# Grouped attention: POOL's query sum ahead of the last pair of scatters, key split, exponentials and one turn moved, and the row turns issued twice

## Chip, cores and metric

One core of one Trainium2 chip runs the whole program. The metric is the device time of one execution in microseconds (us).

## The reference, cut to what matters

The model is two layers on x of shape (16, 512, 128). The change touches only the attention half of the first layer's feed-forward block (`_L0_ffn_ref`), with the router behind it:

```
h = rmsnorm(layernorm(x), ln1_w)
q, k, v = h @ Wq (16 heads of 8), h @ Wk, h @ Wv (4 heads of 8), rope on q and k
attn = softmax(causal(q k^T / sqrt(8)))        # each k, v head serves 4 q heads
h = clip(x + (attn v) @ Wo, -100, 100)
flat = rmsnorm(h, ln2_w); probs = softmax(flat @ Wr); top 2 of 8 experts
```

Behind it come the experts' products, a second attention with eight blocks, and a ternary feed-forward. All sixteen sequences of 512 tokens go through each stage before the next stage begins.

## The kernel before, in words

`grouped_attention` (lines 52 to about 1115) is written by hand for five engines: `pe_program`, `act_program`, `pool_program`, `dve_program` and `sp_program` give each engine one order of work, and semaphores tie them. It is a software pipeline over the NB = 16 sequences. Each program loops `for b in range(-1, NB + 2)` and inside it over eight steps `s`. In one step PE computes the scores of one pair of heads of sequence b and, 11 pairs ahead, the scores from which DVE takes the row maxima. Other parts of the step serve other sequences: c = b + 1 (maxima turned and stored), c2 = b + 2 (its q and k are rotated, split in three bf16 parts and stored), c3 = b + 3 (statistics, normalising, projection), p = b - 1 (output projection, clip, rows for the experts) and r = b - 2 (router and scatters).

What sets the order around the change:

- PSUM: `S` has six banks, used as three pairs in turn. `score(n, part)` and `max_scores(m, part)` alternate, three of each in a step, so each of them waits until the pair was emptied: by `exponentials` on ScalarE or by `take_max` on DVE. `M` is one bank for all small products (`turn_x`, `project_q`, `sum_k`, `turn_o`, `turn_h`, `route` and so on); `bank_free` waits for whoever reads the one before.
- The query chain: `cosines` and `sines` (DVE, lines 775 and 781) fill `rotA` and `rotB`, `rotate` (POOL, line 659) adds them, `split_q` (DVE, lines 804 to 808) makes two bf16 parts and `third_q` (POOL, line 663) the last. The key chain: `sum_k` (PE), `copy_sum` (ScalarE), `split_k` (DVE, lines 793 to 797), `third_k` (POOL, line 668).
- SP's queue, in this order for c2: `store_q`, which waits for `third_q` (lines 1028 to 1032), `store_k` (1038 to 1040), `load_q` (1047) when q's stores have landed, `load_k` (1054) when k's have. They go through DRAM, to bring heads on the partitions that the scores need. PE waits for both loads in `max_scores` at step 4 of b, where the maxima of sequence b + 2 begin.
- POOL also normalises (`scales`, `normalise`), scales the residual, clips, makes the rows for the experts and issues eight indirect DMAs for each sequence (`scatter`, line 716: two choices of expert, four tiles of 128 tokens), in pairs at steps 4, 5, 6 and 7.

Of the kernel before, what the change touches and what calls it, by code (L numbers as in the profile page):

```python
# [46 lines left out]
def grouped_attention(nc, C, XT, H, G, R, NB):  # L47
# [15 lines left out]
    with ExitStack() as ctx:  # L63
# [154 lines left out]
        def pe_program(pe):  # L218
# [86 lines left out]
            def turn_h(r):  # L305
                bank_free()
                pe.wait_ge(row_ready, r + 1)
                for t in range(NT):
                    last = pe.transpose(M[:, t * P:(t + 1) * P], rows[:, r % 2, t, 0:P],
                                        C["ident"][:, :])  # L310
                last.then_inc(h_turned, 1)
                taken[0] = (h_copied, r + 1)
# [116 lines left out]
            for b in range(-1, NB + 2):  # L429
                p, c, c2, c3, r = b - 1, b + 1, b + 2, b + 3, b - 2  # L430
                for s in range(8):
# [16 lines left out]
                        turn_o(b, 0)  # L448
                    if s == 5 and exists(c):
                        turn_max(c)  # L450
                    if s == 6 and exists(b):
                        turn_o(b, 1)
                    if s == 7 and exists(c3):
                        project_qs(c3)
                    if scanning:
                        max_scores(m, 0)
                    if weighing and s % 2 == 0:
                        pe.wait_ge(probs, 6 * group + 6)
                        if group:
                            pe.wait_ge(o_copied, group)  # L460
                        weigh(group, FIRST[0])
# [31 lines left out]
        def act_program(act):  # L493
# [88 lines left out]
            for b in range(-1, NB + 2):  # L582
                p, c, c2, c3, r = b - 1, b + 1, b + 2, b + 3, b - 2
                for s in range(8):
                    n = 8 * b + s + 1
                    attending = 0 <= n < 8 * NB
                    if s == 0 and exists(p):
                        copy_o(p, 2)
                    if s == 2 and exists(p):
                        copy_o(p, 3)  # L590
                    if s == 4 and exists(b):
                        copy_o(b, 0)
                    if s == 6 and exists(b):
                        copy_o(b, 1)
                    if attending:
                        exponentials(n, 0)
                    if s == 1 and exists(r):
                        copy_h(r)
                    if s == 5 and exists(c):
                        copy_max(c)  # L600
                    if attending:
                        exponentials(n, 1)
                    if s == 0 and exists(c2):
                        copy_sum(c2)
                    if s == 2 and exists(c2):
                        copy_v(c2)
                    if s == 2 and exists(r):
                        ratios(r)
                    if s == 3 and exists(p):
                        copy_yT(p)  # L610
                    if s == 5 and exists(c3):
                        copy_xT(c3)
                    if attending:
                        exponentials(n, 2)
                    if s == 6 and exists(p):
                        squares(p)

        def pool_program(pool):
# [109 lines left out]
            pool.memset(v12[:, :, :, :, VD:VD + 1], 1.0).then_inc(zeroed, 1)  # L728
            first_residual()
            residual(1)  # L730
            for b in range(-1, NB + 2):
                p, c2, c3, r = b - 1, b + 2, b + 3, b - 2
                for s in range(8):
                    if s == 0 and exists(c2):
                        rotate(c2)
                    if s == 1 and exists(c2):
                        third_q(c2)
                        third_k(c2)
                    if s == 3 and 2 <= c3 < NB:
                        scales(c3)  # L740
                        normalise(c3)
                    if s == 5 and 1 <= c3 < NB:
                        residual(c3)
                    if s == 5 and exists(p):
                        clip(p)
                    if s == (5 if p == NB - 1 else 6) and exists(p):
                        make_rows(p)
                    if s == 4 and exists(r):
                        weigh_rows(r)
                    if s >= 4 and exists(r):  # L750
                        scatter(r, s // 6, ((0, 1), (2, 3))[s % 2])
            for half in range(2):
                pool.wait_ge(scattered[half], 16 * 2 * NT * (NB // 2))

        def dve_program(v):
# [226 lines left out]
            for b in range(-1, NB + 2):  # L982
                p, c, c2, c3, r = b - 1, b + 1, b + 2, b + 3, b - 2
                for s in range(8):
# [3 lines left out]
                        combine(p, 2)  # L988
                    if s == 2 and exists(p):
                        combine(p, 3)  # L990
                    if s == 3 and exists(r):
                        place(r)
                    if s == 4 and exists(b):
                        combine(b, 0)
                    if s == 6 and exists(b):
                        combine(b, 1)
                    if s == 7 and exists(c3):
                        sines(c3)
                    if scanning:
                        take_max(m, 0)  # L1000
                    if scanning:
                        take_max(m, 1)
                    if s == 0 and exists(c2):
# [6 lines left out]
                        rotate_k(c3)  # L1010
                    if scanning:
                        take_max(m, 2)
                    if s == 0 and exists(c2):
                        split_k(c2)
                    if s == 1 and exists(r):
                        choose(r)
                    if s == 2 and 2 <= c3 < NB:
                        measure(c3)
                    if s == 3 and exists(c):
                        shift(c)  # L1020
            make_plan()

        def sp_program(sp):
# [2568 lines left out]
```

## Time and profile before

| | us |
|---|---|
| median of 3 runs | 3304.95 (3292.81 to 3307.48) |
| the profiled execution, whole | 3274.55 |
| its span | 3272.8 |
| PE busy in the span | 2983.6 |
| DVE busy | 2458.4 |
| ScalarE busy | 2327.2 |
| POOL busy | 2020.2 |

Busy time is the sum over instructions; the span runs from the first to the last instruction. The profiled execution is some 30 us shorter than the median of the runs. Grouped attention is the stretch from about 540 to 1340 us.

### The profile page before, as it was taken

What the parts mean: (1) busy time and instruction counts of PE and PEld (TensorE: products, weight loads), DVE (VectorE), ACT (ScalarE), POOL (GpSimd) and SP (SyncE); (2) the same over time, 40 slices, a digit from 0 to 9 for tenths busy, and PEclk for the clock granted to TensorE, in tenths of its full rate; (3) what the DMA queues carried; (4) which work ended last, traced back from release to release, by engine and by line L of the source; (5) the groups of instructions that cost most, each with busy time, mean ns of one, the idle gap of its engine ahead of it and who ended that gap; (6) DMA issues with size and microseconds to landing.
All of it is one profiled execution on the core that took longest, in us unless ns stands there. A gap on an engine that the chain in (4) does not pass through costs nothing. (4 is left out here: it accounts for less than half of the span.)

```text
span 3272.8 us, 66154 instructions
## 1 busy us (share of the span) xinstructions
PE 2983.6 (91%) x22290; PEld 1870.3 (57%) x22290; DVE 2458.4 (75%) x6927; ACT 2327.2 (71%) x3599; POOL 2020.2 (62%) x2351
## 2 busy tenths in 40 slices
PE   6999997898888988488679999999999999999979
PEld 3554554344444443377536666666666666666658
DVE  5666666888777774366468888888888888888867
ACT  5787773466555657243258999999999999999933
POOL 4454453355555543466547787878787878787745
PEclk8999998899999999699889999999999999999989
DMA  4444434312331220475330000000000000000001
GB/s 122 123 111 102 127 98 94 66 46 58 68 68 45 65 68 18 119 241 162 98 103 1 7 11 1 16 1 16 1 16 1 16 1 16 1 7 11 1 14 40
DMA packets 178774, 178.31 MB, mean 54 GB/s; under 512 B 18667, under 2 KB 159174, under 8 KB 178341
## 3 DMA queue, kind: packets, MB, share of 16 engines
q1 hardware_dynamic: 169348, 157.14, 18.6%
q0 software_dynamic: 9088, 16.94, 1.5%
q8 instruction: 179, 2.93, 0.4%
q14 instruction: 159, 1.29, 0.1%
HBM read 99.82 MB, written 75.95 MB: 54 GB/s over the span
## 5 line engine op out<-in xcount | busy, mean ns | idle before, releaser
L3092 PE MATMUL lb_FF<-lb_h,lb_w 128*128 128x512 f32 x1024 | 501.9, 593 | 0.0
L3325 DVE TENSOR_SCALAR lb_z<-lb_M,lb_mv,lb_rstd 128x128 f32<-128x128 f32 x1024 | 345.2, 399 | 3.3 <-POOL lb_rstd L3247 3.0
L3210 ACT ACTIVATE lb_h<-lb_H,lb_prm 128x512 f32<-128x512 f32 x512 | 326.0, 695 | 2.6 <-PE lb_H L3083 2.6
L3247 POOL TENSOR_TENSOR lb_rstd<-lb_rstd,half 128x4 f32<-128x4 f32 x256 | 260.5, 1018 | 36.9 <-issue 0.9
L3077 PE MATMUL lb_H<-lb_x1s,lb_w 128*128 128x512 f32 x512 | 273.6, 534 | 0.0
L1661 POOL TENSOR_SCALAR_AFFINE_SELECT da_PT<-da_PT 128x1024 f32<-128x1024 f32 x128 | 146.2, 1148 | 192.3 <-ACT da_PT L1587 192.3
L3092 PEld LDWEIGHTS lb_FF<-lb_h,lb_w 128*128 128x128 f32 x1024 | 193.3, 189 | 91.1 <-issue 61.5
L566 ACT ACTIVATE ga_PT<-ga_S 128x384 f32<-128x384 f32 x256 | 111.6, 488 | 184.5 <-PE ga_S L377 184.4
L3317 DVE BATCH_NORM_STATS2 lb_stats<-lb_M 128x6 f32<-128x128 f32 x1024 | 227.2, 285 | 14.3 <-PE lb_M L3036 8.9
L1592 ACT ACTIVATE da_PT<-da_SY 128x1536 f32<-128x1536 f32 x128 | 185.2, 1447 | 72.7 <-PE da_SY L1441 71.8
L2405 POOL DMA_INDIRECT moe_ys<-moe_y,moe_dest x156 | 160.7, 1030 | 111.2 <-DVE moe_y L2287 65.1
L3078 PE MATMUL lb_H<-lb_x1s,lb_w 128*128 128x512 f32 x512 | 202.6, 396 | 0.0
L3083 PE MATMUL lb_H<-lb_x1s,lb_w 128*128 128x512 f32 x512 | 201.8, 395 | 0.0
L1453 PE MATMUL da_O<-da_PT,da_V 128*32 128x128 f32 (+2 forms) x3584 | 191.5, 326 | 2.6 <-DVE da_oT L1824 2.1
L3265 POOL CAST lb_x1s<-lb_x 128x512 fp32r<-128x512 f32 x128 | 78.2, 611 | 175.4 <-DVE lb_x L3350 175.4
L819 DVE TENSOR_REDUCE ga_bm<-ga_S 128x8 f32<-128x1024 f32 x128 | 156.1, 1219 | 36.9 <-PE ga_S L401 32.5
L3258 POOL TENSOR_TENSOR lb_xs<-H,lb_xs 128x512 fp32r<-128x512 f32 x128 | 169.2, 1321 | 18.4 <-issue 0.2
L816 DVE TENSOR_REDUCE ga_bm<-ga_S 128x8 f32<-128x1024 f32 x128 | 156.1, 1220 | 31.4 <-PE ga_S L401 29.4
L3268 POOL TENSOR_TENSOR lb_x1s<-lb_x,lb_x1s 128x512 fp32r<-128x512 f32 x128 | 163.5, 1278 | 20.5 <-issue 20.5
L3279 POOL TENSOR_TENSOR lb_y<-lb_ao,H 128x512 f32<-128x512 f32 x128 | 165.5, 1293 | 16.2 <-ACT lb_ao L3197 13.2
L3291 POOL TENSOR_TENSOR lb_y<-lb_ff,lb_x 128x512 f32<-128x512 f32 x128 | 164.6, 1286 | 8.4 <-PE lb_M L3036 5.3
L3191 ACT ACT_TABLE_LOAD x131 | 168.1, 1283 | 2.3
(445 smaller groups left out, 8786.6 us busy)
## 6 DMA issues: line engine op xcount, KB each, us to landing
moe_w<-experts_dram SPq DMA_DIRECT2D x39, 384.0 KB
da_qT<-da_stq SPq DMA_DIRECT2D x64, 192.0 KB, 3.8
da_kT<-da_stk SPq DMA_DIRECT2D x64, 192.0 KB, 4.4
moe_x<-moe_xs SPq DMA_DIRECT2D x39, 260.0 KB
tc_g<-moe_ys SPq DMA_DIRECT2D x32, 256.0 KB
ga_q<-ga_stq SPq DMA_DIRECT2D x20, 384.0 KB, 6.1
lb_split<-moe_parts SPq DMA_DIRECT2D x8, 896.0 KB
da_stq<-da_parts SPq DMA_DIRECT2D x16, 384.0 KB, 2.4
```

The lines of the kernel that those rows point to most:

```text
L1453: last = pe.matmul(O[32 * c:32 * c + 32, q0:q0 + cols], V[:, (n // 4) % 2, j, 2 * (n % 4) + c % 2, :], PT[:, (2 * n + c // 2) % RING, c % ...
L1592: act.activation(PT[:, n % RING, :, 512:HEAD_COLS], SY[:, :, :].rearrange("p a n -> p (a n)").rearrange("p (i n) -> p i n", i=2), ACT.Exp, ...
L3077: pe.matmul(H[:, k % 2, :], w1[:, 0, k, :], x1s[:, 0, :], start=True, stop=False)
L3078: pe.matmul(H[:, k % 2, :], w1[:, 1, k, :], x1s[:, 0, :], start=False, stop=False)
L3083: pe.matmul(H[:, k % 2, :], w1[:, 0, k, :], x1s[:, 1, :], start=False, stop=True).then_inc(h_filled, 1)
L3092: pe.matmul(FF[:, :], w2[:, k, :], h[:, k, :], start=(k == 0), stop=(k == KC - 1)).then_inc(ff_filled, 1)
L3191: act.preload_act_table_set("gelu_apprx_tanh_and_others")
L3210: act.activation(h[:, k, :], H[:, k % 2, :], ACT.Gelu_apprx_tanh, bias=col(FB1 + k, i)).then_inc(h_ready, 1)
L3247: pool.tensor_tensor(out[:, :], out[:, :], C["half"][:, 0:NT], ALU.pow).then_inc(done, 1)
L3258: pool.tensor_tensor(part_of_x(i, 1), state(i), part_of_x(i, 0).bitcast(F32), ALU.subtract).then_inc(xs_ready, 1)
L3317: v.bn_stats(stats[:, t, :], M[:, t * P:(t + 1) * P])
L3325: last = v.tensor_scalar(z[:, t, :], M[:, t * P:(t + 1) * P], mv[:, t, 0:1], rstd[:, t:t + 1], ALU.subtract, ALU.mult)
```

## The change

It moves work within four programs. On PE `turn_h` issues its four transposes twice, with the same inputs and the same output, and `turn_o(b, 1)` goes behind the first `max_scores` of step 6. On ScalarE the third group of exponentials goes ahead of `copy_yT` and `copy_xT`. On POOL `rotate` of a sequence runs in step 7 of the pass before, between the last two pairs of scatters, and not after them; `third_k` goes ahead of `third_q`, `clip` ahead of `residual`, the second pair of scatters from step 5 to step 4, the third from step 6 to step 7. On DVE `split_k` goes behind the first maximum of step 1, `combine(b, 1)` behind the first maximum of step 6; `measure` and `sines` are written a step later and a step earlier.

```diff
@@ turn_h (PE)
-                for t in range(NT):
+                for t in [*range(NT)] * 2:
                     last = pe.transpose(M[:, t * P:(t + 1) * P], rows[:, r % 2, t, 0:P],
@@ pe_program
-                    if s == 6 and exists(b):
-                        turn_o(b, 1)
                     if s == 7 and exists(c3):
                         project_qs(c3)
                     if scanning:
                         max_scores(m, 0)
+                    if s == 6 and exists(b):
+                        turn_o(b, 1)
@@ act_program
+                    if attending:
+                        exponentials(n, 2)
                     if s == 3 and exists(p):
                         copy_yT(p)
                     if s == 5 and exists(c3):
                         copy_xT(c3)
-                    if attending:
-                        exponentials(n, 2)
@@ pool_program
+            rotate(1)
             for b in range(-1, NB + 2):
                 p, c2, c3, r = b - 1, b + 2, b + 3, b - 2
                 for s in range(8):
-                    if s == 0 and exists(c2):
-                        rotate(c2)
                     if s == 1 and exists(c2):
                         third_q(c2)
+                    if s == 0 and exists(c2):
                         third_k(c2)
...
+                    if s == 5 and exists(p):
+                        clip(p)
                     if s == 5 and 1 <= c3 < NB:
                         residual(c3)
-                    if s == 5 and exists(p):
-                        clip(p)
...
-                    if s >= 4 and exists(r):
-                        scatter(r, s // 6, ((0, 1), (2, 3))[s % 2])
+                    if s == 4 and exists(r):
+                        scatter(r, 0, (0, 1))
+                    if s == 4 and exists(r):
+                        scatter(r, 0, (2, 3))
+                    if s == 7 and exists(r):
+                        scatter(r, 1, (0, 1))
+                    if s == 7 and 2 <= c3 < NB:
+                        rotate(c3)
+                    if s == 7 and exists(r):
+                        scatter(r, 1, (2, 3))
@@ dve_program
+                    if s == 3 and 2 <= c3 < NB:
+                        measure(c3)
                     if s == 3 and exists(r):
                         place(r)
                     if s == 4 and exists(b):
                         combine(b, 0)
+                    if scanning:
+                        take_max(m, 0)
+                    if s == 1 and exists(c2):
+                        split_k(c2)
                     if s == 6 and exists(b):
                         combine(b, 1)
-                    if s == 7 and exists(c3):
-                        sines(c3)
-                    if scanning:
-                        take_max(m, 0)
...
-                    if s == 0 and exists(c2):
-                        split_k(c2)
                     if s == 1 and exists(r):
                         choose(r)
-                    if s == 2 and 2 <= c3 < NB:
-                        measure(c3)
                     if s == 3 and exists(c):
                         shift(c)
+                    if s == 6 and exists(c3):
+                        sines(c3)
```

## Rows read from the trace of the kernel before

**Rows 1.** Windows by stage: us, busy us of each engine, granted clock, DMA share, GB/s
```profile
540.00:1340.00 800.00, 676.91 (x7788) 338.02 (x7784) 591.04 (x1259) 448.13 (x1070) 390.42 (x537) 0.91 0.25 58
```

**Rows 2.** Windows of one sequence and of two stretches in it
```profile
812.30:859.60 47.30, 42.37 (x489) 20.96 (x488) 37.32 (x80) 27.94 (x70) 25.73 (x35) 0.93 0.27 61
...
828.90:835.10 6.20, 6.17 (x50) 2.66 (x52) 5.16 (x22) 2.28 (x4) 0.06 (x1) 0.50 0.84 173
...
837.40:842.30 4.90, 4.18 (x70) 2.33 (x67) 4.60 (x18) 3.44 (x9) 2.25 (x6) 1.00 0.18 35
```

**Rows 3.** Timeline of DVE, steps 0 and 1: start, us, line, operation [idle before, releaser]
```profile
821.32 1.23 DVE L819 TENSOR_REDUCE ga_bm<-ga_S 128x8 f32<-128x1024 f32 x1 [1.00 <-PE ga_S L401]
823.29 0.43 DVE L804 CAST ga_partsQ<-ga_rotA 128x512 bf16<-128x512 f32 x1 [0.74 <-POOL ga_rotA L659]
...
825.50 0.99 DVE L793 CAST ga_partsK<-ga_restK 32x512 bf16<-32x512 f32 x1
826.57 0.68 DVE L795 TENSOR_TENSOR ga_restK<-ga_restK,ga_partsK 32x512 f32<-32x512 f32 x1
827.33 0.42 DVE L797 CAST ga_partsK<-ga_restK 32x512 bf16<-32x512 f32 x1
827.67 1.21 DVE L816 TENSOR_REDUCE ga_bm<-ga_S 128x8 f32<-128x1024 f32 x1
```

**Rows 4.** Timeline of PE, the same steps
```profile
819.77 0.38 PE L401 MATMUL ga_S<-g_k,g_q 48*128 48x384 bf16 x4
...
823.15 0.66 PE L309 MATMUL ga_M<-ident,ga_rows 128*128 128x128 f32 x4
...
825.64 0.39 PE L377 MATMUL ga_S<-ga_q,ga_k 51*128 51x384 bf16 x4 [0.50 <-DVE ga_bm L823]
...
828.93 0.40 PE L377 MATMUL ga_S<-ga_q,ga_k 51*128 51x256 bf16 x2 [1.69 <-DVE ga_bm L816]
```

**Rows 5.** Timeline of POOL: first two scatters of four, sum, thirds
```profile
817.05 1.11 POOL L716 DMA_INDIRECT moe_xs<-ga_rows,slot  x1 [0.80 <-issue]
818.47 0.96 POOL L716 DMA_INDIRECT moe_xs<-ga_rows,slot  x1 [0.30 <-issue]
...
821.98 1.28 POOL L659 TENSOR_TENSOR ga_rotA<-ga_rotA,ga_rotB 128x512 f32<-128x512 f32 x1
825.07 1.15 POOL L663 TENSOR_TENSOR ga_partsQ<-ga_rotB,ga_partsQ 128x512 bf16<-128x512 f32 x1 [1.81 <-DVE ga_partsQ L808]
827.82 1.14 POOL L668 TENSOR_TENSOR ga_partsK<-ga_restK,ga_partsK 32x512 bf16<-32x512 f32 x1 [1.60 <-DVE ga_partsK L797]
```

**Rows 6.** Timeline of SP's queue, in this sequence and the first
```profile
826.25 0.38 SPq L1028 DMA_DIRECT2D ga_stq<-ga_partsQ  x1
...
830.35 0.90 SPq L1047 DMA_DIRECT2D ga_q<-ga_stq  x2
...
565.03 0.37 SPq L1028 DMA_DIRECT2D ga_stq<-ga_partsQ  x1
...
569.09 0.95 SPq L1047 DMA_DIRECT2D ga_q<-ga_stq  x2
```

**Rows 7.** Two lines of DVE by source: ns min/median/max, first and last start
```profile
L793 DVE CAST ga_partsK<-ga_restK x15: 951/993/1001, 564.3 to 1203.7; 32x512 bf16<-32x512 f32 x15
...
L2297 DVE COPY moe_weight<-moe_x x39: 155/160/451, 1369.3 to 1611.2; 128x4 f32<-128x4 f32 x39
```

**Rows 8.** Timeline of PE at steps 3 and 4, and in the first sequence
```profile
841.15 0.28 PE L377 MATMUL ga_S<-ga_q,ga_k 51*128 51x256 bf16 x2 [0.33 <-DVE ga_bm L816]
...
843.42 0.39 PE L347 MATMUL ga_S<-identb,half_masks 64*128 64x256 bf16 x4
...
578.26 0.61 PE L347 MATMUL ga_S<-identb,half_masks 64*128 64x256 bf16 x4 [5.13 <-DMA ga_k<-ga_stk]
```

**Rows 9.** Timeline of PE at step 6 and at the stage's end
```profile
806.61 0.63 PE L281 MATMUL ga_M<-ident,ga_oT 128*128 128x128 f32 x4 [0.37 <-ACT ga_oT L527]
...
1326.99 1.09 PE L309 MATMUL ga_M<-ident,ga_rows 128*128 128x128 f32 x4 [6.10 <-POOL ga_rows L686]
```

More of the change, by code:

```diff
@@ L990, in dve_program @@
                         combine(p, 3)
+                    if s == 3 and 2 <= c3 < NB:
+                        measure(c3)
                     if s == 3 and exists(r):
```

## The prediction

> **What bounds the kernel now.** I read the windows by stage first [rows 1]: the diff touches grouped_attention alone, and that stage holds 800.00 us of the 3272.8 us span. In it TensorE (PE) is busy 676.91 us, VectorE (DVE) 591.04, ScalarE 448.13, POOL 390.42. No engine is full; PE and DVE hand six PSUM banks back and forth, and each waits for the other in turn.
>
> Then the windows of one sequence [rows 2]. A full one (eight steps of the inner loop, s = 0 to 7) takes 47.30 us with a mean granted clock of 0.93. Where the missing share lies the next row shows: from 828.90 to 835.10 the granted clock is 0.50, the lower of the two levels (1.2 GHz), with PE busy 6.17 of 6.20 us. At full clock that is 3.1 us of work.
>
> DVE's timeline ahead of that stretch [rows 3] is one chain. The second maximum of step 0 waits 1.00 us for PE and ends at 822.55; the query split waits 0.74 for POOL's sum; then DVE runs without a gap: split_q, third maximum, split_k from 825.50 to 827.67, and only then step 1's first maximum, which ends at 828.89. PE's timeline [rows 4] shows its other side: PE waits 0.50 us for the third maximum and 1.69 us for that first one, and the half clock follows. POOL's timeline [rows 5]: four scatters from 817.05 on (two are shown), then the sum, 821.98 to 823.26, then the third bf16 parts of q and k. SP's timeline [rows 6]: q is stored from 826.25, loads of q from 830.35, those of k behind them.
>
> **The change, step by step, in a full sequence.** All times are on the clock of the sequence shown. Two moves are none: measure at the end of step 2 and at the head of step 3 is the same place in DVE's order, and so is sines from step 7's head to step 6's tail. They cost 0.
>
> *Sum ahead of the last two scatters.* POOL ends its second scatter at 819.43; the sum then runs to about 820.7 (1.28 us) and is 2.5 us earlier. The wait of 0.74 is gone. PE's completions also come late beside scatters: the last matmul of the second maximum starts before 820.15, yet DVE starts at 821.32 [rows 3, 4], and with three scatters in this stretch gone I give DVE 0.9 of that 1.00 back. split_q starts at about 821.4 instead of 823.29, PE at step 1 at 822.0 instead of 822.6.
>
> *Row turns twice.* Four transposes more. Their spacing in the group of four at 823.15 (0.66 us for four) [rows 4] bounds this by 0.66; PE overlaps them, and I take 0.44. PE gets to step 1's first maximum at 823.6 and DVE can start on it at 824.25, 0.6 us after it is free. So the double turn lies on this chain, but the whole chain is not the end, as below.
>
> *split_k behind step 1's first maximum.* That maximum runs at 824.25 to 825.5 instead of 827.67, so PE's 1.69 us wait goes. What is late next is the second maximum: it is now behind split_k. Here a term shrinks. split_k is 0.99 + 0.68 + 0.42; its first cast takes 0.99 in all 15 sequences [rows 7], although the same cast on four times the partitions takes 0.43 [rows 3], and POOL's third_q (825.07 to 826.22) runs beside it [rows 5]. third_q now stands behind third_k and can't run there, so I take the cast at 0.42: split_k lasts 1.6, to 827.1, the second maximum to 828.3, and PE, done at 827.4, waits 0.9 instead of 1.69 + 0.50.
> The Trainium skill (SBUF — State Buffer, "Who interferes with whom") says that VectorE casts and GpSimd hold a shared port pair as an exclusive lock; the 0.99 agrees. The same rule speaks against the change, since the last two scatters now run beside split_q's casts.
>
> What a row of this kind shows: a DVE copy in the stage that gathers experts, beside scatters, takes 0.160 us in the median and 0.451 at most [rows 7], 0.3 more. Two casts beside two scatters are 0 to 0.6 us, and the 0.6 us that DVE waits for PE hides it. If a cast waits for a whole scatter (0.96) it is up to 1.5, of which 0.9 shows.
>
> *third_k ahead of third_q: the term that I take to decide.* SP stores q first. q's third part was ready at 826.22 and is now behind third_k, which waits for split_k: 827.1 + 1.14 + 1.15 = 829.4, that is 3.2 us later. Store to load takes 3.6 (4.1 before, when SP was still issuing k's stores), so the loads start at 833.1 instead of 830.35: +2.8 us. PE needs q and k of the new sequence at step 4's first maximum, 843.42 before [rows 8]. How long the loads take is seen in the first sequence, where PE did wait for them: load of q issued 569.09, PE freed at 578.26 after a wait of 5.13 [rows 6, 8], 9.1 us. Before, they were thus there at 839.5, 3.9 us early. After, at 842.2. Meanwhile DVE's chain brings PE to that point 2.8 us sooner, at 840.6. So PE waits about 1.6 us for DMA at step 4, and of the 2.8 us won in steps 0 to 3 only 1.2 are left there. Behind that point PE, not DVE, is late, so its small waits for DVE in steps 4 and 5 shrink (one of 0.33 at step 3 is shown [rows 8]); I take 0.23 for them, with bounds 0 and 0.5.
>
> *turn_o and combine of step 6 behind the maximum.* PE's wait of 0.37 for ScalarE's copy [rows 9] goes, since the maximum fills it; combine ends ahead of the projection that needs its bank. -0.37.
>
> *Scatters of step 5 next to those of step 4; exponentials ahead of copies; clip ahead of residual; thirds on POOL.* ScalarE and POOL have room (448 and 390 of 800 us) [rows 1]; the late completions move from step 6 to steps 4 and 5. Bounds -0.4 to +0.4, value 0, because DVE has both signs of slack there.
>
> Sum without the clock: -1.2 - 0.23 - 0.37 = -1.8 us a sequence.
>
> *The clock.* The old half-clock stretch lay behind waits of 0.50 and 1.69 us. The new one at step 1 (0.9) may be too short for it; between 837.40 and 842.30, with a wait of 0.33 [rows 8], the clock stayed at 1.00 [rows 2]. But the DMA wait of 1.6 us is about as long as the 1.69 and has DVE-bound waits ahead of it. I expect the half clock behind it in most sequences. Six us of it cost 3.1, and step 4 on is PE's; three cost 1.5. Allowing for some sequences without it I take 1.3. What it gives back at steps 1 and 2 is in the 2.8 us already, and ends in the DMA wait.
>
> Net -0.5 us for each of the 12 sequences whose steps hold all of this (b = 2 to 13), -6. The two before lack scatters and router: 0. The first, b = -1, is pure loss: split_k starts 1.1 us later, q is stored at 569.4 instead of 565.03, and PE already waits for these loads [rows 8]; bounds 0 and +4.3, taken +3.5, near the upper end since a DVE idle of about 1 us is all that lies between. In the drained end the turn of the last sequence takes 1.09 us at half clock [rows 9]; twice it is +0.9. Sum: -6 + 3.5 + 0.9 = -1.6, call it -2.
>
> The profiled execution took 3274.55 us, 1.75 around its span; it becomes 3273. The median of the runs is 3304.95, 30 us above it, so the same -2 gives **3303**.
>
> **The rivals.**
> 1. *The loads come in time.* If PE's lag or the DVE chain is otherwise than I have it, 3 us a sequence stay: 12 x 3.3 = -40, +4.4 at the ends, 3269. For: before, the margin was 3.9 us. Against: +2.8 on one side and -2.8 on the other overrun it.
> 2. *The DMA wait is there but the clock holds.* 12 x -1.8 + 4.4 = -17: 3288. For: a wait of 0.33 us did nothing. Against: the 1.69.
> 3. *Slower.* The half clock comes at step 4 with its whole six us (2.8 lost, after 0.3 of slack) and split_q's casts wait for scatters, which puts the loads 0.9 later: -1.8 + 2.8 + 0.9 = +1.9 a sequence, 12 x 1.9 + 4.4 = +27: 3332. It decides from the point where clock and casts together cost over 1.8 us. For: PE is busy 6.17 of 6.20 us in the old stretch, all of it stretched work. Against: the cast row's 0.3 us.
> 4. *Nothing is moved that matters*, the waits only change names: 3305 (+-5).
>
> **How the numbers follow.** A measurement of this kernel can tell about 0.5%, 16.5 us, from no change. Chances: my case 0.40, rival 1 0.20, rival 2 0.17, rival 3 0.13, rival 4 0.10. Faster by over 0.5%: rival 1, most of rival 2 and a little of mine, 0.32. Slower: rival 3 and some of mine, 0.18. Within: 0.50. My case's own range is 3290 to 3316. The range takes in rival 1 and goes half way to rival 3: 3266 to 3322.
>
> **What would show it.** PE's rows at step 4 show waits for DMA, up to 1.6 us each (right), or none (rival 1). split_k's first cast is 0.42 (right) or 0.99. The row turn has eight transposes and the maximum of step 1 starts ahead of split_k. SP's first store of q stands behind third_k's end by 1.2 us. PE's granted clock: 0.5 at step 4 rather than at step 1. The first load wait grows from 5.1 to about 9 us. Wrong would be a stage of 800 us that shrinks by over 20 or grows by over 15.

## The result, and the profile after

| | before | after |
|---|---|---|
| median of 7 runs, same chip | 3292.81 us (3284.39 to 3307.48) | 3321.56 us (3311.59 to 3328.55) |
| profiled execution, whole | 3274.55 | 3328.55 |
| its span | 3272.8 | 3326.8 |
| grouped attention, to DVE's plan for the experts | 539.8 to 1347.0: 807.2 | 540.6 to 1387.5: 846.9 |

The ratio is 1.008, 95% interval 1.006 to 1.0099: 28.8 us slower by the medians. The forecast was practically no change (3303); the time lies just inside the edge of its range (3322), and the direction was missed. The two profiled executions are extremes, before's below all seven of its runs and after's the longest of its seven, so their difference of 54 us overstates the change.

Where the 54 us lie: 5.3 ahead of the first exponentials (48.8 became 54.1), 32.0 in sequences 0 to 13, 5.6 in the last two. From the last scores to the end of the experts' products it is 14.2 more (323.9 became 338.1), and the rest gives some 3 back. DVE's plan, by which the table ends the stage, comes 3.1 us sooner behind the last scores, but SP's first load of the experts' rows 2.6 later (1355.58 and 1401.81 us), so the drained end gives nothing back. The code of the experts is unchanged, and the same stretch takes 332.8 to 339.7 us in the six other profiles from chips as slow as this one: the profile of before was short there, and most of the 18 us by which it undercuts its median can lie there rather than in grouped attention.

A full sequence takes 48.98 us in the mean, 46.78 before. By steps, in the mean of the twelve full sequences (b = 2 to 13; a step runs from PE's masks for one pair of scores to the next), and beside it the time lost to the half clock, which is the stretch times the share of the clock not granted:

| us a sequence | before | after | forecast |
|---|---|---|---|
| steps 0 to 3 | 25.3 | 24.0 (-1.3) | -2.8 |
| step 4, with the wait for the loads | 5.7 | 8.6 (+2.9) | +1.6 wait, +1.3 clock |
| steps 5 and 6 | 10.6 | 11.2 (+0.6) | -0.6 |
| step 7 | 5.1 | 5.1 | 0 |
| lost to the half clock, steps 0 to 3 | 2.7 | 2.4 | |
| the same, step 4 | 0 | 2.1 | |
| the same, steps 5 and 6 | 0 | 0.6 | |

The half clock takes 5.1 us of a full sequence after and 2.7 before. These 2.4 us more are about as much as the whole sequence is longer (2.2).

The windows of the changed kernel's stage, of a stretch at step 4 of the sequence that starts at 1134.06, and of another full sequence (from 983.47) with a stretch at its steps 2 and 3 (columns as in [rows 1, 2]):
```profile
540.60:1387.50 846.90, 713.90 (x7852) 361.40 (x7852) 591.68 (x1273) 446.49 (x1070) 395.70 (x543) 0.86 0.24 55
1158.90:1165.70 6.80, 5.85 (x38) 3.16 (x40) 3.50 (x6) 1.15 (x3) 5.75 (x8) 0.51 0.04 13
983.50:1034.50 51.00, 46.84 (x496) 23.55 (x492) 36.81 (x80) 27.89 (x68) 25.73 (x35) 0.83 0.25 57
994.90:1008.50 13.60, 13.25 (x108) 6.71 (x110) 9.49 (x39) 4.25 (x10) 3.39 (x8) 0.50 0.79 161
```
The counts differ by 64 matmuls, the second row turns (the window of [rows 1] ends 7 us before the stage does); DVE's work is the same. The granted clock of the stage fell from 0.91 to 0.86, and PE's busy time rose with it. The second row is the half clock at its new place, step 4. The last row is the half clock at the old place: it did not go. PE's wait at the head of step 2 is 0.98 to 1.08 us in all twelve full sequences, and in eight of them the half clock sets in with it or just behind it, as in the sequence from 983.47; in the other four, the one from 1134.06 among them, it does not:
```profile
995.25 0.61 PE L347 MATMUL ga_S<-identb,half_masks 64*128 64x256 bf16 x4 [1.03 <-DVE ga_bm L828]
...
1145.81 0.39 PE L347 MATMUL ga_S<-identb,half_masks 64*128 64x256 bf16 x4 [1.01 <-DVE ga_bm L828]
```
So the rows that follow show a sequence in which the forecast for steps 0 to 3 came true, and they are not typical in that.

DVE's timeline, steps 0 and 1 of a sequence whose step 0 starts at 1134.06 (816.56 in [rows 3]):
```profile
1137.69 1.23 DVE L828 TENSOR_REDUCE ga_bm<-ga_S 128x8 f32<-128x1024 f32 x1 [0.32 <-PE ga_S L401]
1138.83 0.42 DVE L813 CAST ga_partsQ<-ga_rotA 128x512 bf16<-128x512 f32 x1
...
1141.83 1.23 DVE L825 TENSOR_REDUCE ga_bm<-ga_S 128x8 f32<-128x1024 f32 x1 [0.71 <-PE ga_S L401]
1142.97 0.41 DVE L802 CAST ga_partsK<-ga_restK 32x512 bf16<-32x512 f32 x1
...
1144.55 1.21 DVE L828 TENSOR_REDUCE ga_bm<-ga_S 128x8 f32<-128x1024 f32 x1
```
The split of q follows its maximum without the old wait of 0.74 and the wait of 1.00 is 0.32. The first cast of split_k takes 0.41 where it took 0.99 [rows 3], and 0.40 to 0.41 in all 15 sequences: POOL is no longer on third_q beside it. That is the shared port of the Trainium skill (SBUF — State Buffer, "Who interferes with whom"), and here row and page agree. The cast at 1138.83 runs beside the scatter of 1138.58 (below) and takes 0.42: I had the same rule speak against the change, and this row shows nothing of it.

POOL's and SP's timelines, the same sequence:
```profile
1137.14 1.27 POOL L659 TENSOR_TENSOR ga_rotA<-ga_rotA,ga_rotB 128x512 f32<-128x512 f32 x1
1138.58 0.99 POOL L716 DMA_INDIRECT moe_xs<-ga_rows,slot  x1 [0.17 <-issue]
...
1144.71 1.14 POOL L668 TENSOR_TENSOR ga_partsK<-ga_restK,ga_partsK 32x512 bf16<-32x512 f32 x1 [3.85 <-DVE ga_partsK L806]
1145.82 1.16 POOL L663 TENSOR_TENSOR ga_partsQ<-ga_rotB,ga_partsQ 128x512 bf16<-128x512 f32 x1
```
```profile
1147.00 0.38 SPq L1037 DMA_DIRECT2D ga_stq<-ga_partsQ  x1
1150.78 0.83 SPq L1056 DMA_DIRECT2D ga_q<-ga_stq  x2
1151.66 0.95 SPq L1063 DMA_DIRECT2D ga_k<-ga_stk  x2
```
q's third part waits behind k's, so q is stored 12.94 us after the start of step 0 (9.69 in [rows 6]) and loaded from 16.72 (13.79). The k loads land at 1159.76. What that meets on PE, and the same in the first sequence:
```profile
1155.63 0.28 PE L377 MATMUL ga_S<-ga_q,ga_k 51*128 51x256 bf16 x2 [0.64 <-DVE ga_bm L825]
...
1157.67 0.63 PE L281 MATMUL ga_M<-ident,ga_oT 128*128 128x128 f32 x4 [0.29 <-ACT ga_oT L527]
1159.85 0.61 PE L347 MATMUL ga_S<-identb,half_masks 64*128 64x256 bf16 x4 [1.55 <-issue]
...
1160.82 1.93 PE L410 MATMUL ga_O<-ga_PT,ga_v 128*32 128x512 f32 x8
...
584.36 0.61 PE L347 MATMUL ga_S<-identb,half_masks 64*128 64x256 bf16 x4 [10.06 <-DMA ga_k<-ga_stk]
```
Inside a sequence the wait bears the name "issue", since it is PE's queue that holds it; that it ends 0.09 us after the landing gives its cause. PE was released in this way in 11 of the 15 sequences, counted by that distance. In the other four the half clock had held PE up for 13.7 us of steps 2 and 3, so that it came 2.0 to 2.9 us behind the landing. In the mean of the full sequences the wait is 1.4 us, at most 3.47. Behind it four mask matmuls take 0.61 where they take 0.39 at full clock [rows 8].

In the stretch behind it POOL now issues four scatters in a row, the first and the last of which are shown, and DVE waits for matmuls:
```profile
1160.92 1.23 DVE L825 TENSOR_REDUCE ga_bm<-ga_S 128x8 f32<-128x1024 f32 x1 [0.83 <-PE ga_S L401]
1168.85 1.23 DVE L825 TENSOR_REDUCE ga_bm<-ga_S 128x8 f32<-128x1024 f32 x1 [1.82 <-PE ga_S L401]
```
```profile
1162.80 1.10 POOL L716 DMA_INDIRECT moe_xs<-ga_rows,slot  x1 [0.29 <-POOL ga_rows L696]
...
1166.74 0.96 POOL L716 DMA_INDIRECT moe_xs<-ga_rows,slot  x1 [0.30 <-issue]
```
Before, the second pair came 3.95 us behind the end of the first, with the residual and the clip between them:
```profile
849.71 0.95 POOL L716 DMA_INDIRECT moe_xs<-ga_rows,slot  x1 [0.31 <-issue]
...
854.61 1.07 POOL L716 DMA_INDIRECT moe_xs<-ga_rows,slot  x1 [0.17 <-issue]
```

### The profile page after: what moved, and what is told of

The parts are those of the page before. It is cut to its first block and busy times, and to the rows that moved or that the text cites. A ratio compares the mean times of both kernels' runs of the same rounds, so it can differ in the third digit from the quotient of the medians.

```text
span 3326.8 us, 66282 instructions
## 1 busy us (share of the span) xinstructions
PE 3017.5 (91%) x22354; PEld 1891.8 (57%) x22354; DVE 2450.4 (74%) x6927; ACT 2326.4 (70%) x3599; POOL 2022.9 (61%) x2351
```

## Experiments

One thing has to be known for all of them. The comparisons fell on chips of two kinds, with one session on each chip. On some the kernel before takes 3293 to 3296 us (A below: two of the experiment chips, and the first comparison), on the others 3227 to 3229 (B). Each ratio is against before on its own chip. The same two programs were profiled on both kinds. The rows show DVE's first and second maximum: busy us and mean ns, then the idle time before them. The kernel before on A, then on B:
```profile
L816 DVE TENSOR_REDUCE ga_bm<-ga_S 128x8 f32<-128x1024 f32 x128 | 156.1, 1220 | 31.4 <-PE ga_S L401 29.4
L819 DVE TENSOR_REDUCE ga_bm<-ga_S 128x8 f32<-128x1024 f32 x128 | 156.1, 1219 | 36.9 <-PE ga_S L401 32.5 <-remote 3.4
```
```profile
L819 DVE TENSOR_REDUCE ga_bm<-ga_S 128x8 f32<-128x1024 f32 x128 | 156.2, 1220 | 25.8 <-PE ga_S L401 23.4
L816 DVE TENSOR_REDUCE ga_bm<-ga_S 128x8 f32<-128x1024 f32 x128 | 156.1, 1220 | 17.0 <-PE ga_S L401 15.1
```
The changed kernel on A, then on B:
```profile
L825 DVE TENSOR_REDUCE ga_bm<-ga_S 128x8 f32<-128x1024 f32 x128 | 156.5, 1223 | 75.4 <-PE ga_S L401 70.2 <-remote 3.1
L828 DVE TENSOR_REDUCE ga_bm<-ga_S 128x8 f32<-128x1024 f32 x128 | 156.3, 1221 | 40.6 <-PE ga_S L401 39.0
```
```profile
L825 DVE TENSOR_REDUCE ga_bm<-ga_S 128x8 f32<-128x1024 f32 x128 | 156.5, 1223 | 53.2 <-PE ga_S L401 51.2
L828 DVE TENSOR_REDUCE ga_bm<-ga_S 128x8 f32<-128x1024 f32 x128 | 156.3, 1221 | 35.9 <-PE ga_S L401 33.5
```
The operations take the same on both; DVE waits longer for PE on A. In A's traces such a wait can end long after the matmul. Where DVE stands idle for a maximum whose last matmul ended within 1.5 us after a scatter's start, it starts 0.74 us behind that end in the mean of before, 0.63 in the change and 1.48 in e16, by 3.3 at most; with no scatter that near, 0.04 to 0.06. In B's twelve traces it is 0.04 everywhere. Below, this is called a late completion.

All results (stage, to DVE's plan, and mean full sequence from each kernel's own profile, us; the kernel before has 807.2 and 46.78 on A):

| | kind | ratio to before, 95% | stage | sequence |
|---|---|---|---|---|
| change, first comparison | A | 1.008 [1.006, 1.0099] | 846.9 | 48.98 |
| change again (e7) | B | 1.0048 [1.0035, 1.0061] | 810.3 | 46.66 |
| before again, one run (e8) | B | | 811.6 | 47.14 |
| k first alone (e2) | B | 1.0032 [1.0018, 1.0046] | 805.8 | 46.36 |
| split_k alone (e4) | B | 0.9981 [0.9971, 0.9991] | 800.5 | 46.14 |
| q first (e1) | B | 0.9899 [0.988, 0.9917] | 769.5 | 43.79 |
| q first, again (e12) | B | 0.9905 [0.9889, 0.9922] | | 43.95 |
| q first, third time (e16) | A | 1.0045 [1.0029, 1.0061] | 829.5 | 48.22 |
| keep clock (e3) | B | 0.9998 [0.9987, 1.0009] | 797.9 | 45.51 |
| keep clock, again (e14) | B | 0.9992 [0.9981, 1.0002] | | 45.38 |
| single turn (e5) | B | 1.0035 [1.0023, 1.0047] | 805.1 | 46.34 |
| q first, single (e6) | B | 0.988 [0.9866, 0.9894] | 760.2 | 42.94 |
| the same, again (e13) | B | 0.9879 [0.986, 0.9898] | | 42.94 |
| the same, third time (e17) | A | 1.0038 [1.0019, 1.0056] | 820.8 | 47.91 |
| e6 with split_k later (e9) | A | 1.0105 [1.0087, 1.0124] | 844.7 | 49.45 |
| e6 with the sum last (e10) | A | 1.0132 [1.0099, 1.0165] | 860.6 | 50.69 |
| the same, again (e18) | A | 1.0139 [1.0113, 1.0165] | 857.9 | 50.62 |
| e6 with early statistics (e11) | A | 0.996 [0.9942, 0.9979] | 803.3 | 45.55 |
| the same, again (e15) | B | 0.9856 [0.9838, 0.9874] | 753.0 | 42.18 |

**Order of the thirds.** The change, but q's third part ahead of k's (e1, e12, e16):
```diff
-                    if s == 1 and exists(c2):
-                        third_q(c2)
                     if s == 0 and exists(c2):
+                        third_q(c2)
+                    if s == 1 and exists(c2):
                         third_k(c2)
```


> The changed kernel with third_q ahead of third_k again. Theory A (q's third part, behind split_k and third_k, stores q late, PE waits for the loads at step 4 and falls to half clock there): q is stored at about 5 us earlier in each sequence, no DMA wait at step 4, a full sequence takes 43.5 to 45 us in place of 48 to 51, ratio to before 0.983 to 0.992. Theory B (the double turns, the scatters next to each other and the sum between scatters cost it): the sequence stays at 47.5 us or more and the ratio at 1.003 to 1.008.

On B it is 1% faster than before, and 1.5% (3241.81 to 3197.9 us, 44 us) faster than the change. These two times come from two chips of kind B, where before took 3228.53 and 3226.83. POOL and SP in it, then PE at step 4, in the sequence whose step 0 starts at 812.83:
```profile
819.65 1.16 POOL L663 TENSOR_TENSOR ga_partsQ<-ga_rotB,ga_partsQ 128x512 bf16<-128x512 f32 x1
823.33 1.14 POOL L668 TENSOR_TENSOR ga_partsK<-ga_restK,ga_partsK 32x512 bf16<-32x512 f32 x1 [2.52 <-DVE ga_partsK L806]
```
```profile
820.84 0.38 SPq L1037 DMA_DIRECT2D ga_stq<-ga_partsQ  x1
825.86 0.90 SPq L1056 DMA_DIRECT2D ga_q<-ga_stq  x2
```
```profile
836.31 1.07 PE L281 MATMUL ga_M<-ident,ga_oT 128*128 128x128 f32 x4 [0.29 <-ACT ga_oT L527]
837.31 0.60 PE L347 MATMUL ga_S<-identb,half_masks 64*128 64x256 bf16 x4
```
q is stored 2.5 us ahead of the start of k's third part, and PE goes into step 4 without a wait for the loads (the 1.07 and 0.60 show that its clock is half here too, with no wait longer than 0.64, 0.38 and 0.29 us in the 3 us ahead; it is so in five of the twelve full sequences, and the stage's mean is 0.92). The repetition on B:

> The changed kernel with third_q ahead of third_k, again. On a chip with late completions: if the late store is the whole cause of the harm, 0.988 to 0.993 as on the other chip; if the late completions carry part of it, steps 0 and 2 to 5 keep some of it and the ratio is 0.996 to 1.004. On a chip without them 0.989 to 0.991 again.

0.9905: the same. The first edit alone, in the kernel before (`third_k(c2)` ahead of `third_q(c2)`, e2):

> The kernel before with third_k ahead of third_q and nothing else. Theory A: q's third part comes 3.3 us later, which the old margin of about 3.9 us at step 4 just holds in most sequences, and split_k's first cast falls from 0.99 to 0.42 us; the first sequence's wait for loads grows by 3.3 us. Ratio 0.996 to 1.004. If the order of the thirds costs by itself, whatever the margin: ratio 1.006 or more, with DMA waits at step 4.

1.0032, clearly slower, though the sequences of its profile, 8 us below its median, are no longer than before's: without the earlier sum and split_k, PE arrives later, and its wait for the loads at step 4 is 0.8 us in the mean of the full sequences, with seven of over 1 us among the 15; in e7 the mean is 1.15. Its front, from the stage's start to the first exponentials, is 54.4 us. So the order of the thirds costs 0.3% by itself on B and 1.5% once the rest of the change brings PE there earlier.

**The clock behind the wait.** The change, with the four transposes that precede the wait issued four times, so that PE works where it waited (e3, e14):
```diff
-                for t in range(NT):
+                for t in [*range(NT)] * (4 if g == 0 else 1):
```


> The changed kernel with the turn of step 4 (turn_o of group 0) issued four times instead of once, which fills 1.3 us of PE's wait for the loads with transposes. Theory A with the clock as its larger term: PE still reaches the first maximum of the new sequence when the loads have landed, but at full clock; steps 4 and 5 lose 2 to 3 us less in a sequence, ratio to before 0.997 to 1.003. If the wait itself is the cost and the clock costs little: ratio 1.007 or more, since PE has 1.3 us more work.

PE's timeline at step 4:
```profile
848.76 1.94 PE L281 MATMUL ga_M<-ident,ga_oT 128*128 128x128 f32 x16 [0.29 <-ACT ga_oT L527]
851.57 0.40 PE L347 MATMUL ga_S<-identb,half_masks 64*128 64x256 bf16 x4 [0.87 <-issue]
852.12 1.06 PE L410 MATMUL ga_O<-ga_PT,ga_v 128*32 128x512 f32 x8
```
The masks behind the wait take 0.40, not 0.61, and the attention's eight matmuls 1.06, not 1.93: full clock, with the loads as late as ever. 0.9998 against the change's 1.0048 on the same kind: 16 us by the ratios, about 1.2 a sequence by the profiles, belong to the half clock and not to the wait itself. Not all of it lies behind the wait: of the 1.15 us between the profiles of e7 and e3, step 4 has 0.66, with the 1.3 us of extra transposes in it, and steps 0 to 3 have 0.48. Repeated:

> The changed kernel with the turn of step 4 four times, again. If the half clock behind the DMA wait is the larger term on a chip with late completions too: ratio 0.998 to 1.004, against 1.008 of the changed kernel. If it is not: 1.008 or more. On a chip without late completions 0.999 to 1.001 again.

0.9992, on B again, so what the half clock costs on A was not tested in this way. Useless work made the kernel faster by what it kept of the clock.

**split_k behind the first maximum, alone**, in the kernel before (e4):
```diff
@@ dve_program, behind take_max(m, 0)
+                    if s == 1 and exists(c2):
+                        split_k(c2)
...
-                    if s == 0 and exists(c2):
-                        split_k(c2)
```


> The kernel before with split_k behind the first maximum of step 1 and nothing else (third_q stays ahead of third_k, the sum behind all scatters, the row turns single). Theory A: q is stored at its old time, no DMA wait; PE's wait of 1.69 us for the first maximum goes, one of about 1.4 us for the second takes its place, so 0.6 to 1.5 us a sequence are won: ratio 0.994 to 0.999. If split_k's place alone brings the harm of the change: ratio 1.004 or more.

0.9981: a gain of 0.2%, by the interval real. The edit is good and small.

**Single row turns** (e5: the change with `for t in range(NT):` in `turn_h`; e6, e13, e17: the same in q first).

> The changed kernel with the row turns issued once. Theory A: the double turn is 0.44 us on the chain that ends in q's store, and its work does not reach step 4; so the DMA wait of step 4 shrinks by 0.4 us at most and stays, and steps 1 and 2 see the half clock at least as often: 2 to 6 us less than the changed kernel in all, ratio to before 1.003 to 1.008 where the changed kernel has 1.008. Theory B (the double turns are the harm): the ratio falls to 1.000 or below.

> The changed kernel with third_q ahead of third_k and the row turns issued once. If the double turns hold the clock up at steps 1 and 2 and are worth it: a ratio above that of the same kernel with double turns (0.990), 0.992 to 0.996, with half clock at steps 1 and 2 in more sequences. If they are only 0.44 us on DVE's chain: 0.987 to 0.989, a sequence 0.3 to 0.5 us shorter.

1.0035 against the change's 1.0048, and 0.988 against 0.9899; in both pairs the intervals overlap. In e5 the step of the turn is 5.77 us, with the double turn 6.21: exactly the 0.44 of the forecast. I see nothing that it buys back on B.

> The same with single turns. On a chip with late completions the half clock comes more easily at steps 1 and 2; if the double turns hold it off there, this one is slower than the one with double turns (by up to 1%). On a chip without them 0.987 to 0.989 again.

0.9879, the same as e6.

**The change and before again** (e7, e8), on the same chip as e5 and e6:

> The changed kernel itself, beside the others on one chip. Ratio 1.006 to 1.010 as in the first comparison. On a chip where PE's completions are not late beside scatters, steps 0 and 5 lose less and 1.003 to 1.007 is to be expected, with the same DMA wait at step 4.

> The kernel before itself, for its trace on this chip. Theory A rests on PE and DVE taking turns: the stage takes 800 to 807 us, a full sequence 46.4 to 47 us with half clock at step 1 or 2. If PE's completions are on time beside scatters here, step 0 takes 5.4 us, not 6.05.

The change is slower on B too, by half as much as on A. Before's one profiled run took 3237.29 us, 10 over its median there, so the sequences of its profile (47.14) are up to 0.8 us longer than usual ones and can't be held against the 46.66 of the change. It shows what is different on B: at step 0
```profile
823.80 1.23 DVE L819 TENSOR_REDUCE ga_bm<-ga_S 128x8 f32<-128x1024 f32 x1 [0.32 <-PE ga_S L401]
827.09 0.43 DVE L804 CAST ga_partsQ<-ga_rotA 128x512 bf16<-128x512 f32 x1 [2.06 <-POOL ga_rotA L659]
```
the maximum waits 0.32 for PE where it waited 1.00 [rows 3], and the wait moves to POOL's sum, 2.06 us.

**Parts of the best version so far, taken apart**, all from e6. split_k behind the second maximum of step 1 (e9):
```diff
-                    if s == 1 and exists(c2):
-                        split_k(c2)
                     if scanning:
                         take_max(m, 1)
+                    if s == 1 and exists(c2):
+                        split_k(c2)
```


> The changed kernel with third_q first and single turns (0.988), and split_k one maximum later still, behind the second maximum of step 1. PE's wait of 1.0 us at the head of step 2 goes. If DVE's chain from split_q to step 4 is the bound, PE only waits later for it: ratio 0.986 to 0.990. If that wait of PE is the bound: 0.983 to 0.986. k is ready 1.2 us later; were that to overrun the margin of the loads, DMA waits at step 4 and 0.991 or more.

It ran on A: 1.0105, against 1.0038 of e6's code on A (another chip, e17); none of the expected ranges held. The waits of its PE from 600 to 1250 us (us in all, times, longest):
```profile
PE ga_M L281 <- DVE ga_logit L879: 15.2, 12, 1.5
```
In e17 PE has no such wait of over 0.8 us in all. I read it so: split_k now holds up the copy of the logits, and PE's turn of the output needs that bank. Later is worse.

The sum behind all the scatters, as in the kernel before (e10, e18):
```diff
-                    if s == 7 and 2 <= c3 < NB:
-                        rotate(c3)
                     if s == 7 and exists(r):
                         scatter(r, 1, (2, 3))
+                    if s == 7 and 2 <= c3 < NB:
+                        rotate(c3)
```


> The changed kernel with third_q first and single turns (0.988), and POOL's query sum behind all scatters of the sequence, as before the change. If the early sum carries most of what is won beside the order of the thirds: split_q waits 1.5 to 2 us for it, a sequence is 1.0 to 1.5 us longer, ratio 0.991 to 0.994. If only the place of split_k won: 0.988 to 0.989.

> third_q first, single turns, the query sum behind all scatters. Late completions: 1.010 to 1.016 as before, with half clock at steps 1 to 3 in every sequence. Without them: split_q waits 1.5 to 2 us for the sum, 0.991 to 0.995; if the early sum is worth little there, 0.988 to 0.990.

1.0132, outside the first range, and 1.0139, inside the second; on the same chip as e17, 1.0139 to 1.0038: the early sum is worth 1% there, 35 us. Without it nine of the twelve full sequences in e10 have half clock over 10.2 us of steps 2 and 3 and again over 3.4 behind. Of the parts timed alone this is the strongest. On B it was not timed by itself.

The statistics a step earlier still, at the end of step 7 of the pass before (e11, e15):
```diff
-                    if s == 3 and 2 <= c3 < NB:
+                    if s == 3 and b == -1:
                         measure(c3)
...
+                    if s == 7 and b + 4 < NB:
+                        measure(b + 4)
```


> The changed kernel with third_q first and single turns (0.988), and the statistics of a sequence (1.24 us of DVE) taken at the end of step 7 of the pass before, where DVE waits for PE, and not in step 3. If DVE's chain bounds steps 0 to 3, a sequence is 0.6 to 1.2 us shorter: ratio 0.983 to 0.986. If PE or the loads bound it, nothing is won (0.987 to 0.990).

> third_q first, single turns, statistics at the end of step 7, again. On a chip with late completions 0.994 to 0.998 again. On one without: DVE's chain in steps 1 to 3 is 1.2 us shorter, 0.983 to 0.986.

0.996 on A, short of the expected 0.983 to 0.986, and 0.9856 on B, within it. That is faster than before and than the change on both kinds, and the best version here, 3183.17 us on B and 3281.15 on A. On A the gain does not lie where it was expected: against e17 steps 0 to 3 take 0.9 us more, step 4 takes 1.0 more, and steps 5 and 6 take 9.55 us for 13.81. The next part says why that matters.

The other moves (exponentials ahead of the copies, clip ahead of the residual, turn_o and combine of step 6, the two pairs of scatters) were never timed one by one.

**Does the order of the thirds explain A?** q first and q first with single turns, on A:

> The changed kernel with third_q ahead of third_k, a third time. On a chip with late completions: 0.988 to 0.993 if the late store is the whole cause, 0.996 to 1.004 if late completions carry part of the harm. On a chip without them 0.989 to 0.991.

> The same with single turns. Late completions: above e16 if the double turns hold the clock up there, 0.2% below it if they are only work. Without late completions 0.987 to 0.989.

Not wholly. 1.0045 (just above the second expected range) and 1.0038 (0.07% below e16, not 0.2%, with intervals that overlap), where B gave 0.9905 and 0.9879, though the loads are in time here too. From the change's 1.008 it is 0.35%, with intervals that touch. The stage of e16 took 829.5 us, against the change's 846.9:
```profile
540.50:1370.00 829.50, 697.76 (x7852) 352.32 (x7852) 588.49 (x1273) 447.64 (x1070) 395.32 (x543) 0.88 0.25 56
```
while q first on B has
```profile
539.70:1309.20 769.50, 664.46 (x7852) 340.70 (x7852) 587.96 (x1273) 448.19 (x1070) 395.48 (x543) 0.92 0.27 60
```
Where the time goes shows in step 5 of e16: POOL with the first and last of its four scatters, then PE, then DVE.
```profile
854.17 1.10 POOL L716 DMA_INDIRECT moe_xs<-ga_rows,slot  x1 [0.29 <-POOL ga_rows L696]
...
858.10 0.96 POOL L716 DMA_INDIRECT moe_xs<-ga_rows,slot  x1 [0.30 <-issue]
```
```profile
856.64 0.39 PE L401 MATMUL ga_S<-ga_k,ga_q 48*128 48x128 bf16 x8
858.61 0.66 PE L231 MATMUL ga_M<-ident,ga_xn 128*128 128x128 f32 x4
861.24 0.28 PE L377 MATMUL ga_S<-ga_q,ga_k 51*128 51x256 bf16 x2 [1.98 <-DVE ga_bm L825]
```
```profile
855.80 0.68 DVE L832 TENSOR_REDUCE ga_bm<-ga_S 128x2 f32<-128x512 f32 x1
859.96 1.23 DVE L825 TENSOR_REDUCE ga_bm<-ga_S 128x8 f32<-128x1024 f32 x1 [3.48 <-PE ga_S L401]
```
The last matmul of the maximum ends at about 857.03. DVE is free since 856.5, and starts at 859.96, as the four scatters come to their end at 859.06: 2.9 us late. PE then waits 1.98 us for that maximum, and half clock follows. The change put this row of four there; before had two scatters, the residual and the clip, and two scatters more.

The sums over steps 5 and 6, in the mean of the full sequences, fit it:

| us | before | change | q first | q first, single | with early statistics |
|---|---|---|---|---|---|
| A, steps 5 and 6 | 10.64 | 11.22 | 13.59 | 13.81 | 9.55 |
| B, steps 5 and 6 | 10.03 | 9.50 | 9.51 | 9.53 | 9.50 |

With q first steps 5 and 6 take 4.1 us more on A than on B, 49 us in twelve sequences, which is the whole distance between 1.0045 and 0.990. With the early statistics POOL normalises sooner and the same row of four ends 2.9 to 5.4 us ahead of step 5, and steps 5 and 6 cost on A what they cost on B. Single sequences say the same: on A step 5 takes 4.4 to 4.8 us wherever the row has ended by its start, in e11 in all twelve, and in the change and in e16 in the last full sequence (b = 13) too. In the eleven other sequences of e16 the row ends 3.4 to 5.3 us into step 5, and the step takes 6.1 to 7.9. On B it takes 4.4 to 4.5 with the row at either place.

## Why the prediction was wrong, step by step

**Right.** q's store and loads: forecast 3.2 and 2.8 us later; against the start of step 0, 3.25 and 2.93. The DMA wait at step 4, forecast as up to 1.6 us in each sequence: 1.55 in the one shown and 1.4 in the mean, but none in four of the 15 and 3.47 at most. The cast: 0.42 forecast, 0.41. Double turn: 0.44. The casts of split_q beside scatters: no price, as I took it. Rival 3's second half did not come; its first did. And the counterpart: with q first and nothing to wait for, B's sequence is 43.79, near rival 1's price of about 3 us off the 46.78 of before's profile (whose 3269 would be 0.989 of the 3304.95; e1 0.9899). That the two agree so well is in part luck, since the 46.78 is from A.

The forecast was -0.5 us for a full sequence, the profiles have +2.2. The 2.7 between them lie in two of its steps, 1.5 and 1.2; a third was wrong in size without moving the sum of its step.

**Wrong, and the largest, 1.5 us: the half clock of steps 1 and 2 was taken as gone.** "The new one at step 1 (0.9) may be too short for it", and "What it gives back at steps 1 and 2 is in the 2.8 us already". The wait came about as forecast, 1.0 us, but in eight of the twelve full sequences the half clock came with it: steps 0 to 3 lose 2.4 us to it in the mean, 2.7 before. So they are 1.3 us shorter and not 2.8. In the sequence shown, where the clock held, they are 3.0 shorter, and PE's masks at step 4 run 25.79 us after the start of step 0 for 26.86 before, 1.07 earlier where 1.2 was forecast; in the mean of the full sequences they run 0.4 us later. Why the same wait brings half clock in one sequence and not in the next stays open: in e1, on B, it is four of the twelve.

**Wrong, 1.2 us: "Scatters of step 5 next to those of step 4 ... Bounds -0.4 to +0.4, value 0, because DVE has both signs of slack there".** I had read that completions come late beside scatters, and took back 0.9 us for it at step 0, but priced the same thing at nothing where the scatters went. With the small terms of -0.37 and -0.23, steps 5 and 6 should have been 0.6 us shorter; on A they are 0.6 longer, on B 0.5 shorter. DVE had no slack behind PE at step 5: it stands idle for 1.82 us in the sequence shown and for 3.48 in the one of e16. Late completions work by what follows them, too: 0.6 us of these two steps is half clock that was not there before.

**Wrong in size, though its step came out right: the clock at step 4, "I take 1.3".** The half clock takes 2.1 us of step 4 in the mean on A, 3.4 of its 9.8 us in the sequence shown, and 1.6 on B. The wait was shorter in exchange, and absent where the half clock of steps 2 and 3 had already held PE up, so that step 4 as a whole grew by 2.9 us, as forecast. I had bounded the stretch by the old one (6 us, 3.1) and then taken less than half of that for sequences without it.

**Wrong in size: the first sequence, +3.5.** The load wait grew from 5.13 to 10.06 us, more than the 9 forecast, and the front by 5.3 us on A, above my bound of 4.3, and by some 4 on B. The wait of 1 us of DVE's that I counted as cover was none. The drained end, +0.9 forecast, is 2.6 us longer to SP's first load of the experts' rows.

**What it sums to.** On B the late q store costs 44 us (change to q first), of which the first sequence is about 2 (fronts of 53.2 and 51.2), the rest of the front's loss being there also with q first; the half clock that e3 took away is 16 of it. The other edits together bring 29 to 31 us of gain there (e12, e1). On A those same edits lose 16 with q first (e16), although the early sum among them is worth 35: by the sums over steps 5 and 6 the row of four scatters and the half clock behind it are the rest. That is read from the traces and from the difference between the kinds, not shown by an edit: none took the second pair of scatters back to step 5 alone. Nor was any edit made that keeps the clock at steps 2 and 3 of the change, so the largest term rests on the traces too. And the change's 1.008 and e16's 1.0045 come from two chips, so the price of the late store on A, 0.35%, is uncertain by as much.

The 30 us between before's profiled execution and its median were a warning that I noted and did not use. As the section on the result shows, most of it can be the experts' stage. Whether the 807.2 us of grouped attention in that one profile are usual for A stays open, since before was profiled there once.

## What to carry to other kernels

Before moving a producer behind another, follow its output to the last reader through every queue: POOL's order set SP's order, which set when PE could enter step 4, and on B the 3.2 us there cost 1.5%, more than the other edits together won. The margin of a load is used up from both sides: whatever makes the consumer earlier eats into it too. If a row shows a cost beside some operation, price it at the operation's new place as well as at the old, and in a row of several count the whole row. And read a term from the mean of many passes: the one sequence that is laid out step by step can be the one in which the clock held.

## What the runs showed of the hardware

- One program takes 3293 us on one chip and 3228 on another, steadily, with equal durations of its operations in grouped attention. In that stage PE's completions come late beside POOL's scatters on the first kind (DVE starts up to 3.3 us behind the matmul that it waits for), and not on the second (0.04); the stage that follows, from the first load of the experts' rows to the end of their products, takes 268 to 281 us on A and 226 to 228 on B. A change that moves indirect DMAs is to be timed on both kinds: q first is 0.990 on one and 1.0045 on the other.
- The length of one wait of PE did not tell whether half clock follows. It came in or just behind the wait of 1.0 us at the head of step 2 in 8 of 12 full sequences of the change on A, in 10 of 12 on B (e7) and in 4 of 12 with q first (e1). With waits of 0.8 to 3.5 us for the loads at step 4 it came in 16 of 16 (change and e7); with q first it came there in 5 of 12 with no wait over 0.64 us just ahead. The time lost to it is 5.1 us of a full sequence of the change on A and 4.3 on B. Twelve extra transposes of 128x128 in place of a wait kept the granted clock high and won 0.5%.
- A 32-partition DVE cast takes 0.99 us beside a POOL operation on two tensors in SBUF and 0.40 to 0.41 without; beside a scatter's issue a 128-partition cast stays at 0.42.
